# x kept in SBUF from the first attention into the cross attention of a decoder kernel

## The chip, the cores and the metric

The kernel runs on one core of a Trainium2 chip. The metric is the device time of one execution in microseconds. Times given as "median" are medians over several runs; the profile is of one further execution. Engines are called PE (TensorE, matmuls), PEld (its weight loads), DVE (VectorE), ACT (ScalarE), POOL (GpSimd) and SP (SyncE, which here only issues DMAs). Names such as SPq or PEq are an engine's instruction queue.

## What is computed

Two post-norm decoder layers over x of 8 x 256 rows with 512 columns, float32. Each step adds a branch to x and normalises the rows:

```
x = _layernorm(x + _L0_attn_ref(x, ...))        # quantised projections, 32 heads
x = _layernorm(x + _L0_xattn_ref(x, ctx_2048, mask))
x = _layernorm(x + _L0_ffn_ref(x, ...))         # base feed-forward and two of eight low-rank experts
x = _layernorm(x + _L1_attn_ref(x, ...))
x = _layernorm(x + _L1_xattn_ref(ctx, ctx, x, ...))
x = _layernorm(x + _L1_ffn_ref(x, ...))
```

The change lies in the end of the first line and in the second. The branch of the second line is one attention without projections, with D = 512:

```
scores = einsum('bsd,bmd->bsm', hidden_states, memory_tokens) * scale
scores = where(memory_mask, scores, -1e30)
attn = softmax(scores, axis=-1)
readout = einsum('bsm,bmd->bsd', attn, memory_tokens)
```

## The kernel before

The program is a list of stages, each a block in which the five engines run their own instruction lists and meet through semaphores. Between two stages all engines wait for each other. Every engine takes its list strictly in order, and a wait holds everything behind it on that engine. The order is written out by hand in loops, so the code order is the execution order of an engine. The 2048 rows of x are 16 tiles of 128 rows (NT = 16, index n); a block b of 256 rows has TB = 2 tiles.

**attention0_finish** (L710) is the last stage of the first attention: it quantises the attention's output cf, multiplies by the output weights, adds x and normalises. A loop over i works on block i, with these steps:

- POOL `take_bias` (L790) subtracts a bias from a block of cf, three blocks ahead; DVE `scale` (L850) multiplies it; ACT `rounded` (L916) adds the rounding constant; DVE `quantise` (L875) writes the bf16 operand quant, two blocks ahead.
- PE multiplies quant by the weights into one of four accumulators (L961, L966).
- DVE scales the accumulator of each tile into one of eight row buffers r (L890, signal y_ready), POOL adds x from a2_xt (L803, sum_ready), DVE takes mean and variance one block later (L904, L905, var_ready), POOL adds epsilon and takes the power -0.5 (L811, L813, root_ready), and DVE normalises the row in r two blocks later (L896, x1_ready).
- SP stores each finished row tile to the DRAM tensor x1 (L783). The stage ends when all stores have landed (L785).

In the trace the tiles a2_xt, a2_r and so on are called a_xt and a_r.

**cross_attention** (L1014) reads x1 back. A loop over s runs a pipeline over the tiles: at step s, PE transposes tile s of x (L1147, into c_pxf), multiplies scores of tile s-1 (L1156, c_psc), the output of tile s-3 (L1165, c_pout), and transposes the probabilities of tile s-2 (L1174, c_ppt), in this order. ACT copies the transposed x (L1186), takes the exponential of tile s-1 (L1193), copies the transposed probabilities of tile s-2 (L1200). DVE masks the scores of tile s-1 and takes their maximum (L1235 to L1238), adds the output of tile s-3 to x (L1249), takes its moments, and normalises tile s-4 (L1260). ACT also issues the stores of x2 (L1209).

SP feeds it: `load_x(b)` (L1090) issues three DMAs for block b, all counted on one semaphore got_x: x from x1 (L1094), the context rows ct (L1096) and the transposed context cf (L1098). There are three buffers, so blocks 0 to 2 are loaded at the start, and a later block b is issued at step 2b-2, once the tile two before it in DVE's additions is done (semaphore added). PE waits for all three DMAs ahead of the transposes of a block's first tile (L1143).

Beside this work the stage prepares the next stage's weights: 20 pieces, each loaded by SP into one of five raw buffers (L1113), rounded to a high part by ACT (L1205) and turned into a low part by DVE (L1265). `pieces_of(s)` (L1037) says which pieces belong to step s: `n * NT // NP == s`, which gives pieces 0 and 1 to step 0 and the last one to step 15. ACT and DVE take a step's pieces at the step's end; the piece that uses the same raw buffer five pieces on is issued by SP after w_low.

Of the kernel before, what the change touches and what calls it, by code (L numbers as in the profile page):

```python
# [15 lines left out]
F32 = mybir.dt.float32  # L16
# [6 lines left out]
P = 128  # L23
# [34 lines left out]
class Maker:  # L58
# [5 lines left out]
    def sb(self, name, shape, dt=F32):  # L64
        return self.ctx.enter_context(self.nc.sbuf_tensor(name, shape, dt))
# [644 lines left out]
def attention0_finish(nc, io, sem, keep):  # L710
# [9 lines left out]
    SPAN = KT * NC  # L720

    with ExitStack() as ctx:
# [27 lines left out]
        xt = mk.sb("a2_xt", [P, NT, D])  # L750
# [7 lines left out]
                 "y_ready", "sum_ready", "tail_steps", "var_ready", "root_ready", "x1_ready")  # L758
        s_ = {n: sem(f"a2_{n}") for n in names}
        got_x = [sem(f"a2_got_x{b}") for b in range(B)]  # L760
        stored = [sem(f"a2_stored{n}") for n in range(RR)]
# [11 lines left out]
        with nc.Block() as block:  # L773
            @block.sync
            def _(sp):
# [5 lines left out]
                for n in range(NT):  # L781
                    sp.wait_ge(s_["x1_ready"], n + 1)
                    sp.dma_start(io["x1"][n * P:(n + 1) * P, :], r[:, n % RR, :]).then_inc(stored[n % RR], 16)  # L783
                for n in range(RR):
                    sp.wait_ge(stored[n], 16 * (NT // RR))  # L785

            @block.gpsimd
            def _(pool):
# [7 lines left out]
                for i in range(B + 1):  # L796
                    for q in range(TB):
                        n = i * TB + q
                        if n < NT:
# [3 lines left out]
                            pool.tensor_tensor(r[:, n % RR, :], r[:, n % RR, :], xt[:, n, :], ALU.add  # L803
# [3 lines left out]
                    for q in range(TB):  # L807
                        n = (i - 1) * TB + q
                        if 0 <= n < NT:
# [3 lines left out]
                            pool.tensor_tensor(stats[:, n, 9:10], stats[:, n, 8:9], keep["neghalf"][:, :], ALU.pow  # L813
                                               ).then_inc(s_["root_ready"], 1)

            @block.vector
            def _(dve):
# [63 lines left out]
                for i in range(B + 2):  # L881
                    if i + 2 < B:
                        scale(i + 2)
                    for q in range(TB):
                        n = i * TB + q
                        if 0 <= n < NT:
                            dve.wait_ge(s_["acc_done"], n + 1)
                            if n >= RR:
                                dve.wait_ge(stored[n % RR], 16 * (n // RR))
                            dve.scalar_tensor_tensor(r[:, n % RR, :], acc[n % RING][:, :], unit_tok[:, n:n + 1], wsrow[:, :],  # L890
                                                     ALU.mult, ALU.mult).then_inc(s_["y_ready"], 1)
                    for q in range(TB):
                        n = (i - 2) * TB + q
                        if 0 <= n < NT:
                            dve.wait_ge(s_["root_ready"], n + 1)
                            dve.tensor_scalar(r[:, n % RR, :], r[:, n % RR, :], stats[:, n, 6:7], stats[:, n, 9:10],  # L896
                                              ALU.subtract, ALU.mult).then_inc(s_["x1_ready"], 1)
                    if i + 2 < B:
                        quantise(i + 2)
                    for q in range(TB):  # L900
                        n = (i - 1) * TB + q
                        if 0 <= n < NT:
                            dve.wait_ge(s_["sum_ready"], n + 1)
                            tl.step(dve.bn_stats(stats[:, n, 0:6], r[:, n % RR, :]))  # L904
# [3 lines left out]
            def _(act):  # L908
# [23 lines left out]
                for b in range(1, B):  # L932
                    rounded(b)
# [80 lines left out]
def cross_attention(nc, io, sem, keep):  # L1014

    NT = N // P
    XT, CT, RAW, HALF = 6, 3, 5, DFF // 2  # L1020
    CUT = ((0, 6), (6, FT))
    ER = E_ * R_
    BLOCKED = 1e30
# [2027 lines left out]
```

## Time and profile before

| | us |
|---|---|
| median of 3 runs | 2139.03 |
| lowest and highest of them | 2136.92, 2142.73 |
| the profiled execution: its time | 2141.15 |
| its span in the trace | 2139.4 |

| engine | busy us | share of the span |
|---|---|---|
| PE | 1819.8 | 85% |
| DVE | 1452.1 | 68% |
| ACT | 956.3 | 45% |
| POOL | 509.6 | 24% |

The shares are means over stages that have different limits. The stages that the change touches, by the trace: attention0_finish from 394.2 to 487.1 us, cross_attention from 487.1 to 615.4 us of the span. A timeline row reads: start, length, engine, source line, operation, what it wrote and read, shapes, count, and in square brackets how long the engine had been idle before it and what ended that. A merged row (x2) spans several instructions.

### The profile page before, as it was taken

Reading aid. Unit: us, or ns where it says so; the run is one execution under the profiler, and the core shown is the slowest. Engines: PE = TensorE matmul, PEld = TensorE weight load, DVE = VectorE, ACT = ScalarE, POOL = GpSimd, SP = SyncE. Lnnn points to the kernel's source line nnn. Section 1 sums busy time; section 2 is a strip of 40 time slices with the busy share of each in tenths; the row PEclk is TensorE's granted clock in tenths of the full one; section 3 lists DMA queues with packets and bytes.
Section 4 is the critical chain, followed back from the end, with each engine's and each line's share of the span. In section 5 each row is a group of like instructions: output and inputs, shape, how many; then the busy total and the mean of one; then the engine's idle time right before and its main releaser. Section 6 shows DMA issues by size and latency. Waiting matters only on the chain. (4 is left out here: it accounts for less than half of the span.)

```text
span 2139.4 us, 32688 instructions
## 1 busy us (share of the span) xinstructions
PE 1819.8 (85%) x12270; PEld 1374.9 (64%) x12270; DVE 1452.1 (68%) x2729; ACT 956.3 (45%) x1614; POOL 509.6 (24%) x503
## 2 busy tenths in 40 slices
PE   4489999765668999999999985999997799857886
PEld 2256665213448999999999975777875577623443
DVE  8478887694745566566566554566665677648997
ACT  3436666402314444444444432433443211259995
POOL 5233331270010010010000001001100388723422
PEclk9679999656889999999999997999998999978998
DMA  5598894217622122222221214211211311030000
GB/s 157 51 98 96 96 97 45 99 66 230 205 79 57 55 64 69 75 67 63 80 72 56 67 48 162 104 70 40 90 60 54 118 50 50 21 123 6 20 22 34
DMA packets 117568, 166.53 MB, mean 78 GB/s; under 512 B 13536, under 2 KB 67680, under 8 KB 115104
## 3 DMA queue, kind: packets, MB, share of 16 engines
q1 hardware_dynamic: 110756, 151.85, 29.9%
q10 hardware_dynamic: 6656, 12.58, 1.6%
q8 instruction: 99, 1.62, 0.4%
q14 instruction: 57, 0.47, 0.1%
HBM read 117.91 MB, written 21.05 MB: 65 GB/s over the span
## 5 line engine op out<-in xcount | busy, mean ns | idle before, releaser
L1583 ACT ACTIVATE f_gate<-f_gu 128x256 f32<-128x256 f32 x264 | 98.2, 381 | 274.3 <-PE f_gu L1449 187.1
L1711 DVE TENSOR_TENSOR f_hid<-f_gate,f_gu 128x256 f32<-128x256 f32 x264 | 108.2, 420 | 162.6 <-ACT f_gate L1583 159.7
L567 DVE TENSOR_REDUCE a_rowmax<-a_ring 128x2 f32<-128x512 f32 x256 | 164.9, 687 | 51.7 <-PE a_ring L649 49.4
L2525 PE MATMUL e_py<-e_kv,e_toep 128*128 128x320 f32 x640 | 174.5, 436 | 7.5 <-DVE e_kv L2549 7.5
L2525 PEld LDWEIGHTS e_py<-e_kv,e_toep 128*128 128x128 f32 x640 | 122.7, 192 | 59.0 <-issue 9.1
L520 ACT ACTIVATE a_prob<-a_sT 128x1024 f32<-128x1024 f32 x128 | 130.6, 1026 | 48.0 <-PE a_sT L638 48.0
L1462 PE MATMUL f_gu<-f_lowh,f_bg 128*128 128x256 f32 x704 | 141.3, 283 | 5.2 <-POOL f_lowl L1368 4.9
L1449 PE MATMUL f_gu<-f_xhi,f_wg 128*128 128x256 f32 x704 | 130.5, 283 | 0.0
L1449 PE MATMUL f_gu<-f_xhi,f_wu 128*128 128x256 f32 x704 | 129.1, 281 | 0.0
L1716 DVE TENSOR_TENSOR f_hl<-f_hid,f_hh 128x768 fp32r<-128x768 f32 (+2 forms) x90 | 84.5, 939 | 55.9 <-ACT f_hh L1629 54.8
L1462 PEld LDWEIGHTS f_gu<-f_lowh,f_bg 128*128 128x128 f32 x704 | 115.6, 191 | 9.7 <-POOL f_lowl L1368 5.2
L1486 PE MATMUL f_pout<-f_wd,f_hh 128*128 128x512 f32 x352 | 111.6, 398 | 0.0
L1449 PEld LDWEIGHTS f_gu<-f_xhi,f_wg 128*128 128x128 f32 x704 | 108.9, 189 | 0.9 <-POOL f_xlo L1364 0.8
L1449 PEld LDWEIGHTS f_gu<-f_xhi,f_wu 128*128 128x128 f32 x704 | 107.8, 188 | 0.0
L2017 PE MATMUL d_ring<-d_xh,d_w 128*128 128x256 f32 x512 | 95.9, 288 | 13.1 <-DVE d_xl L2336 13.1
L1629 ACT ACTIVATE f_hh<-f_hid 128x768 fp32r<-128x768 f32 (+2 forms) x90 | 74.9, 832 | 62.4 <-DVE f_hid L1711 62.4
L1462 PE MATMUL f_gu<-f_lowl,f_bg 128*128 128x256 f32 x352 | 99.5, 283 | 0.0
L1449 PE MATMUL f_gu<-f_xlo,f_wg 128*128 128x256 f32 x352 | 99.4, 283 | 0.0
L1449 PE MATMUL f_gu<-f_xlo,f_wu 128*128 128x256 f32 x352 | 99.0, 281 | 0.0
L649 PE MATMUL a_ring<-a_ks,a_qs 48*128 48x256 f32 x512 | 62.8, 322 | 40.4 <-DVE a_rowmax L567 20.2
L2017 PEld LDWEIGHTS d_ring<-d_xh,d_w 128*128 128x128 f32 x512 | 79.5, 192 | 20.0 <-issue 18.0
L481 POOL TENSOR_TENSOR a_y<-a_y,cb 128x512 f32<-128x512 f32 x48 | 50.0, 1042 | 177.2 <-DVE a_y L549 177.2
(420 smaller groups left out, 4853.5 us busy)
## 6 DMA issues: line engine op xcount, KB each, us to landing
f_entry<-in_WdT SPq DMA_DIRECT2D x89, 256.0 KB
d_staging<-in_w SPq DMA_DIRECT2D x16, 1024.0 KB, 5.5
a_qs<-a_hi SPq DMA_DIRECT2D x64, 128.0 KB, 7.2
a_ks<-a_hi SPq DMA_DIRECT2D x64, 128.0 KB, 6.2
e_toep<-lags SPq DMA_DIRECT2D x32, 256.0 KB, 3.1
f_entry<-in_Bg SPq DMA_DIRECT2D x89, 64.0 KB
f_entry<-in_Bu SPq DMA_DIRECT2D x89, 64.0 KB
cf<-in_xT SPq DMA_DIRECT2D x4, 1024.0 KB, 7.8
```

Source lines behind the costliest of these rows:

```text
L520: act.activation(prob[:, n % 4, :, :, :], sT[n % 2][:, :, :, :], ACT.Exp).then_inc(exp_done, 1)
L567: dve.tensor_reduce(rowmax[:, s % 2, :, e * SLOTS + j], ring[n % RING][:, :].rearrange("p (q t) -> p q t", t=T), AX.X, ALU.max, negate=Tru ...
L649: last = pe.matmul(dst[e][:, q * T:(q + 1) * T], qs[par][rows, pair, q * P:(q + 1) * P], ks[par][rows, pair, :], start=True, stop=True)
L1449: last = pe.matmul(gu[n % 3][:, w, :], ws[hw][:, k, f * P:(f + 1) * P], xs[:, b % 2, k, :], start=(m == 0 and w == 0), stop=(m == 3 * KT - ...
L1462: last = pe.matmul(gu[n % 3][:, w, :], bg[:, n % BR, h, w, :], xs[:, u, j - 1, w, :], start=False, stop=True, skip_group_check=True)
L1486: last = pe.matmul(pout[q][:, :], xs[:, t % 2, 0, cols], wd[:, n % WR, h, :], start=(f == 0 and m == 0), stop=(f == FT - 1 and m == 2))
L1583: act.activation(gate[:, i % 2, :], gu[n % 3][:, 0, :], ACT.Silu).then_inc(s_["gate_ready"], 1)
L1629: act.activation(hh[:, t % 2, lo:hi, :], hid[:, lo:hi, :], ACT.Copy).then_inc(s_["hh_ready"], 1)
L1711: dve.tensor_tensor(hid[:, j, :], gate[:, i % 2, :], gu[n % 3][:, 1, :], ALU.mult).then_inc(s_["hid_ready"], 1)
L1716: dve.tensor_tensor(hl[:, t % 2, lo:hi, :], hid[:, lo:hi, :], hh[:, t % 2, lo:hi, :], ALU.subtract).then_inc(s_["hl_ready"], 1)
L2017: last = pe.matmul(dst[:, f * T:(f + 1) * T], w[hw][:, wi, k, o * P:(o + 1) * P], xs[:, k, :], start=(m == 0), stop=(m == 3 * KT - 1))
L2525: last = pe.matmul(py[n % RING][:, 0:DIAG * BS], toep[:, h % 3, (t - j) * P:(t - j + 1) * P], kv[:, h % 2, :, j, :], start=(j == 0), stop= ...
```

## The change

1. **x stays in SBUF.** The buffer of x in attention0_finish becomes `x_rows1`, allocated so that it outlives the stage, and is handed on in `keep["rows1"]`. POOL's sum is written into it, not into r. Nothing is stored to x1, and cross_attention reads, updates and stores its tiles in this buffer; c_xt and c_r go. `load_x` issues two DMAs, not three.
2. **Where PE waits.** The wait for a block's DMAs moves from ahead of the transposes of its first tile to ahead of its scores, which are one step later.
3. **ScalarE makes the rows.** In attention0_finish the normalisation leaves DVE (L896) for ACT, as one activation with a scale and a bias per row. For the bias, -mean times root, POOL gets a third small operation per tile behind its power. DVE's wait for a row buffer is now on sum_ready, not on a landed store.
4. **Weight pieces two steps on.** `pieces_of` spreads the same 20 pieces over steps 2 to 15 and not over steps 0 to 15.

```
@@ attention0_finish
-                for n in range(NT):
-                    sp.wait_ge(s_["x1_ready"], n + 1)
-                    sp.dma_start(io["x1"][n * P:(n + 1) * P, :], r[:, n % RR, :]).then_inc(stored[n % RR], 16)
-                for n in range(RR):
-                    sp.wait_ge(stored[n], 16 * (NT // RR))
...
-                            pool.tensor_tensor(r[:, n % RR, :], r[:, n % RR, :], xt[:, n, :], ALU.add
+                            pool.tensor_tensor(xt[:, n, :], r[:, n % RR, :], xt[:, n, :], ALU.add
...
                             pool.tensor_tensor(stats[:, n, 9:10], stats[:, n, 8:9], keep["neghalf"][:, :], ALU.pow
+                                               ).then_inc(s_["root_steps"], 1)
+                            pool.wait_ge(s_["root_steps"], n + 1)
+                            pool.tensor_scalar(stats[:, n, 8:9], stats[:, n, 6:7], stats[:, n, 9:10], -1.0, ALU.mult, ALU.mult
                                                ).then_inc(s_["root_ready"], 1)
...
-                                dve.wait_ge(stored[n % RR], 16 * (n // RR))
+                                dve.wait_ge(s_["sum_ready"], n - RR + 1)
...
-                    for q in range(TB):
-                        n = (i - 2) * TB + q
-                        if 0 <= n < NT:
-                            dve.wait_ge(s_["root_ready"], n + 1)
-                            dve.tensor_scalar(r[:, n % RR, :], r[:, n % RR, :], stats[:, n, 6:7], stats[:, n, 9:10],
-                                              ALU.subtract, ALU.mult).then_inc(s_["x1_ready"], 1)
...
-                for b in range(1, B):
-                    rounded(b)
+                rounded(1)
+                for i in range(B + 2):
+                    if i + 2 < B:
+                        rounded(i + 2)
+                    for q in range(TB):
+                        n = (i - 2) * TB + q
+                        if 0 <= n < NT:
+                            act.wait_ge(s_["root_ready"], n + 1)
+                            act.activation(xt[:, n, :], xt[:, n, :], ACT.Identity, bias=stats[:, n, 8:9], scale=stats[:, n, 9:10]
+                                           )
@@ cross_attention
-        return [n for n in range(NP) if n * NT // NP == s]
+        return [n for n in range(NP) if 2 + n * (NT - 2) // NP == s]
...
-                    sp.dma_start(xt[:, at:at + TB, :], io["x1"][b * T:(b + 1) * T, :].rearrange("(n p) f -> p n f", p=P)
-                                 ).then_inc(got_x[b % CT], 16)
...
-                        pe.wait_ge(got_x[n // TB % CT], 48 * (n // TB // CT + 1))
                         if n >= 2:
                             pe.wait_ge(s_["xf_ready"], n - 1)
...
                         pe.wait_ge(s_["xf_ready"], n + 1)
+                        pe.wait_ge(got_x[n // TB % CT], 32 * (n // TB // CT + 1))
```

The instruction order of DVE in a middle iteration of the loop in attention0_finish (cf is the attention's output, a_r the row buffers). Before:

```order
L850 TENSOR_TENSOR cf<-cf,a_inv 128x4x256
L890 SCALAR_TENSOR_TENSOR a_r<-a_acc,a_unit_tok,a_wsrow 128x512 x2
L896 TENSOR_SCALAR a_r<-a_r,a_stats 128x512 x2
L875 SCALAR_TENSOR_TENSOR quant<-cf,a_grow 128x4x256
L904 BN_STATS a_stats<-a_r 128x6
L905 BN_AGGR a_stats<-a_stats 128x2
L904 BN_STATS a_stats<-a_r 128x6
L905 BN_AGGR a_stats<-a_stats 128x2
```

and of the change, the same place (x_rows is the kept buffer):

```order
L849 TENSOR_TENSOR cf<-cf,a_inv 128x4x256
L889 SCALAR_TENSOR_TENSOR a_r<-a_acc,a_unit_tok,a_wsrow 128x512 x2
L874 SCALAR_TENSOR_TENSOR quant<-cf,a_grow 128x4x256
L897 BN_STATS a_stats<-x_rows 128x6
L898 BN_AGGR a_stats<-a_stats 128x2
```

The two normalisations between the scaled accumulators and the quantisation are gone from DVE. POOL in the same iteration, of the change:

```order
L799 TENSOR_TENSOR x_rows<-a_r,x_rows 128x512 x2
L786 TENSOR_TENSOR cf<-cf,a_cbias 128x4x256
L807 TENSOR_SCALAR a_stats<-a_stats 128x1
L809 TENSOR_TENSOR a_stats<-a_stats,neghalf 128x1
L812 TENSOR_SCALAR a_stats<-a_stats 128x1
L807 TENSOR_SCALAR a_stats<-a_stats 128x1
L809 TENSOR_TENSOR a_stats<-a_stats,neghalf 128x1
L812 TENSOR_SCALAR a_stats<-a_stats 128x1
```

Here only the two operations of L812 are new. ACT at the start of cross_attention (c_xf is the transposed x, c_raw a raw weight buffer, f_wa and f_ad high parts of weights). Before:

```order
L1186 ACTIVATE c_xf<-c_pxf 128x512
L1205 ACTIVATE f_wa<-c_raw 128x512 x2
L1186 ACTIVATE c_xf<-c_pxf 128x512
L1193 ACTIVATE c_prob,c_rowsum<-c_score,c_negmax 128x256
L1205 ACTIVATE f_ad<-c_raw 128x768
```

and of the change:

```order
L1184 ACTIVATE c_xf<-c_pxf 128x512 x2
L1191 ACTIVATE c_prob,c_rowsum<-c_score,c_negmax 128x256
L1184 ACTIVATE c_xf<-c_pxf 128x512
L1191 ACTIVATE c_prob,c_rowsum<-c_score,c_negmax 128x256
L1198 ACTIVATE c_probT<-c_ppt 128x256
L1203 ACTIVATE f_wa<-c_raw 128x512 x2
L1184 ACTIVATE c_xf<-c_pxf 128x512
```

The first two weight pieces now stand behind the second tile's exponential, where before they stood behind the first copy of x.

## Rows read from the trace of the kernel before

**Rows 1.** Windows by stretch: length, busy of each engine, clock, DMA share, GB/s.
```profile
core 0: us, PE busy (x) PEld busy (x) DVE busy (x) ACT busy (x) POOL busy (x), PEclk, DMA share, GB/s
417.00:467.30 50.30, 40.12 (x82) 12.37 (x80) 43.07 (x51) 5.96 (x6) 38.40 (x35) 0.50 0.11 42
487.10:508.20 21.10, 6.34 (x21) 4.61 (x21) 2.21 (x5) 2.34 (x4) 0.00 (x0) 0.58 1.00 310
520.80:601.90 81.10, 59.80 (x216) 41.10 (x214) 60.15 (x163) 27.01 (x62) 8.20 (x12) 0.85 0.56 182
```

**Rows 2.** Timeline of DVE, one iteration of attention0_finish.
```profile
451.50 1.40 DVE L890 SCALAR_TENSOR_TENSOR a_r<-a_acc,a_unit_tok,a_wsrow 128x512 f32<-128x512 f32 x2
...
455.27 2.92 DVE L875 SCALAR_TENSOR_TENSOR quant<-cf,a_grow 128x1024 bf16<-128x1024 f32 x1
458.11 0.68 DVE L904 BATCH_NORM_STATS2 a_stats<-a_r 128x6 f32<-128x512 f32 x1
...
459.72 1.19 DVE L850 TENSOR_TENSOR cf<-cf,a_inv 128x1024 f32<-128x1024 f32 x1
460.83 1.41 DVE L890 SCALAR_TENSOR_TENSOR a_r<-a_acc,a_unit_tok,a_wsrow 128x512 f32<-128x512 f32 x2
462.15 2.53 DVE L896 TENSOR_SCALAR a_r<-a_r,a_stats 128x512 f32<-128x512 f32 x2
464.61 1.21 DVE L875 SCALAR_TENSOR_TENSOR quant<-cf,a_grow 128x1024 bf16<-128x1024 f32 x1
```

**Rows 3.** Timeline of POOL, the same iteration.
```profile
455.03 2.08 POOL L790 TENSOR_TENSOR cf<-cf,a_cbias 128x1024 f32<-128x1024 f32 x1
459.10 0.22 POOL L811 TENSOR_SCALAR a_stats<-a_stats 128x1 f32<-128x1 f32 x1 [1.99 <-DVE a_stats L905]
...
459.95 1.04 POOL L811 TENSOR_SCALAR a_stats<-a_stats 128x1 f32<-128x1 f32 x1
...
461.72 2.67 POOL L803 TENSOR_TENSOR a_r<-a_r,a_xt 128x512 f32<-128x512 f32 x2
```

**Rows 4.** Timeline at the two borders of attention0_finish.
```profile
394.24 0.06 DVE L820 MEMSET a_plus<- 128x1 f32 x1 [0.34 <-PEq L450]
...
483.02 0.55 DVE L896 TENSOR_SCALAR a_r<-a_r,a_stats 128x512 f32<-128x512 f32 x1 [0.45 <-POOL a_stats L813]
...
487.14 0.37 SPq L1094 DMA_DIRECT2D c_xt<-x  x1
```

**Rows 5.** Timeline, start of cross_attention; last, ACT's rounding by line, 417 to 467.3 us.
```profile
494.96 1.97 PE L1147 MATMUL c_pxf<-ident,c_xt 128*128 128x128 f32 x8 [23.09 <-DMA c_cf<-in_ctxFM]
496.76 3.78 PE L1156 MATMUL c_psc<-c_cf,c_xf 128*128 128x256 f32 x8
506.03 0.63 ACT L1205 ACTIVATE f_wa<-c_raw 128x512 fp32r<-128x512 f32 x1 [9.32 <-DMA c_raw<-in_AgT]
508.20 0.42 DVE L1235 SCALAR_TENSOR_TENSOR c_score<-c_psc,c_mask 128x256 f32<-128x256 f32 x1
...
L916 ACT ACTIVATE cf<-cf,a_plus 128x1024 f32<-128x1024 f32 x6 | 6.9, 1148 | 42.0 <-DVE cf L850 42.0
```

**Rows 6.** Cross_attention's steps: timeline; waits and one line of 520.8 to 601.9 us; a window.
```profile
520.76 0.42 DVE L1235 SCALAR_TENSOR_TENSOR c_score<-c_psc,c_mask 128x256 f32<-128x256 f32 x1
523.17 0.38 SPq L1094 DMA_DIRECT2D c_xt<-x  x1
529.87 1.12 PE L1147 MATMUL c_pxf<-ident,c_xt 128*128 128x128 f32 x4 [4.26 <-DMA c_cf<-in_ctxFM]
601.92 0.42 DVE L1235 SCALAR_TENSOR_TENSOR c_score<-c_psc,c_mask 128x256 f32<-128x256 f32 x1
...
DVE c_score L1235 <- PE c_psc L1156: 15.9, 5, 4.9
...
L1265 DVE TENSOR_TENSOR f_wu<-c_raw,f_wu 128x704 fp32r<-128x704 f32 x8 | 7.0, 884 | 0.0
...
520.00:525.00 5.00, 5.00 (x22) 3.25 (x21) 4.75 (x14) 2.71 (x6) 0.64 (x1) 1.00 0.37 90
```

More of the change, by code:

```diff
@@ L62, in __init__, with sb @@
         self.nc, self.ctx = nc, ctx
-    def sb(self, name, shape, dt=F32):
-        return self.ctx.enter_context(self.nc.sbuf_tensor(name, shape, dt))
+    def sb(self, name, shape, dt=F32, side="left"):
+        return self.ctx.enter_context(self.nc.sbuf_tensor(name, shape, dt, side=side))
     def ps(self, name, shape, dt=F32):
@@ L720, in attention0_finish @@
     SPAN = KT * NC
+    held = ExitStack()
+    xt = Maker(nc, held).sb("x_rows1", [P, NT, D], side="right")
+    keep["rows1"].update(held=held, rows=xt)
     with ExitStack() as ctx:
@@ L757, in attention0_finish @@
                  "bias_ready", "inv_ready", "cb_ready", "cbpart_ready", "eps_added", "sub_ready", "mul_ready", "round_ready", "quant_ready", "acc_done",
-                 "y_ready", "sum_ready", "tail_steps", "var_ready", "root_ready", "x1_ready")
+                 "y_ready", "sum_ready", "tail_steps", "var_ready", "root_steps", "root_ready")
         s_ = {n: sem(f"a2_{n}") for n in names}
         got_x = [sem(f"a2_got_x{b}") for b in range(B)]
-        stored = [sem(f"a2_stored{n}") for n in range(RR)]
         flat = keep["cf"][:, :, :].rearrange("p k (c t) -> p k c t", t=CHUNK)
@@ L880, in _ @@
                 quantise(1)
-                for i in range(B + 2):
+                for i in range(B + 1):
                     if i + 2 < B:
@@ L903, in _ @@
                             dve.wait_ge(s_["sum_ready"], n + 1)
-                            tl.step(dve.bn_stats(stats[:, n, 0:6], r[:, n % RR, :]))
+                            tl.step(dve.bn_stats(stats[:, n, 0:6], xt[:, n, :]))
                             dve.bn_aggr(stats[:, n, 6:8], stats[:, n, 0:6]).then_inc(s_["var_ready"], 1)
@@ L978, in attention0 @@
         mk = Maker(nc, ctx)
+        keep["rows1"] = {}
         own = dict(keep, ws=mk.sb("ws", [P, 4 * KT]), unit=mk.sb("unit", [P, NC]),
@@ L1019, in cross_attention @@
     NT = N // P
-    XT, CT, RAW, HALF = 6, 3, 5, DFF // 2
+    CT, RAW, HALF = 3, 5, DFF // 2
+    xt = keep["rows1"]["rows"]
     CUT = ((0, 6), (6, FT))
@@ L1037, in pieces_of @@
     def pieces_of(s):
-        return [n for n in range(NP) if n * NT // NP == s]
-    with ExitStack() as ctx:
+        return [n for n in range(NP) if 2 + n * (NT - 2) // NP == s]
+    with keep["rows1"]["held"], ExitStack() as ctx:
         mk = Maker(nc, ctx)
-        xt = mk.sb("c_xt", [P, XT, D])
         ct = mk.sb("c_ct", [P, CT, TB, D])
@@ L1068, in cross_attention @@
         got_x = [sem(f"c_got_x{u}") for u in range(CT)]
-        stored = [sem(f"c_stored{u}") for u in range(4)]
+        stored = sem("c_stored")
         piece_in = [sem(f"c_piece_in{u}") for u in range(RAW)]
@@ L1146, in _ @@
                         for k in range(KT):
-                            last = pe.transpose(pxf[n % 2][:, k * P:(k + 1) * P], xt[:, n % XT, k * P:(k + 1) * P],
+                            last = pe.transpose(pxf[n % 2][:, k * P:(k + 1) * P], xt[:, n, k * P:(k + 1) * P],
                                                 keep["ident"][:, :])
@@ L1208, in _ @@
                         act.wait_ge(s_["x_ready"], n + 1)
-                        act.dma_start(io["x2"][n * P:(n + 1) * P, :], r[:, n % 4, :]).then_inc(stored[n % 4], 16)
-                for n in range(4):
-                    act.wait_ge(stored[n], 16 * (NT // 4))
+                        act.dma_start(io["x2"][n * P:(n + 1) * P, :], xt[:, n, :]).then_inc(stored, 16)
+                act.wait_ge(stored, 16 * NT)
             @block.vector
@@ L1257, in _ @@
                     if 0 <= n < NT:
-                        y = r[:, n % 4, :]
+                        y = xt[:, n, :]
                         dve.wait_ge(s_["root_ready"], n + 1)
```

9 lines of the change are left out of this document (2 added, 7 removed).

## The prediction

> **What bounds the kernel now.** I read the windows first [rows 1], cut at the borders of the two stages that the change touches, then the timelines in them, last the list of waits. Everything after 615.4 us has the same instructions in both kernels, so the sum is made of three stretches only.
>
> In the loop of attention0_finish (417 to 467.3 us) no engine is full: DVE is busy for 43.1 of 50.3 us, POOL for 38.4, PE for 40.1 at half its clock [rows 1]. But an iteration takes 460.83 - 451.50 = 9.33 us [rows 2], and some of the busy time is waiting in disguise. The quantisation L875 took 2.92 us where it ran beside POOL's L790 and 1.21 us where it did not; POOL's tiny L811 took 1.04 us beside DVE's L850 and 0.22 us alone [rows 2, 3]. The starts fit one reading: these operations do not run side by side. L790 ended at 457.11, and the quantisation ended 1.08 us later, at 458.19, as if it had begun then. L904 (one SBUF input) and L890 (which reads PSUM) kept their short times. So POOL and part of DVE take turns, and the loop is bound by a chain that crosses both.
>
> At the start of cross_attention (487.1 to 508.2 us) nothing computes much: DVE 2.2 of 21.1 us, DMA share 1.00 [rows 1]. PE waits for the first block until 494.96. Then ACT waits 9.32 us for the first weight piece, to 506.03, and the first scores wait on DVE behind that piece, to 508.20 [rows 5]. In the body (520.8 to 601.9 us) DVE is busy for 60.15 of 81.1 us [rows 1] and waits 15.9 us in five waits for scores; PE had stood before the transposes of a block's first tile for its DMAs, 4.26 us in one case [rows 6], with the previous tile's scores queued behind them.
>
> **Loop of attention0_finish.** The two normalisations leave DVE: 2.53 us in rows 2, of which most is turn-taking with L803. The freed time does not all come out. POOL's own work in an iteration is the two sums 2.5 (2.67 with a short turn in them), L790 1.9 (2.08 with one), two roots at 0.85 each = 1.7 (from 459.10 to 459.95) [rows 3]. New are two operations like L811, 0.22 us and a gap of 0.08, 0.6 together. To this come DVE's turns for L850 and L875, each about 1.15 us, in which POOL stands: 2.5 + 1.9 + 1.7 + 0.6 + 2.3 = 9.0 us. POOL had 1.99 us of idle time in the iteration, waiting for DVE's variance [rows 3]; that goes, and POOL becomes the bound at 9.0 against 9.33. I take 0.35 us for each of four iterations, 1.4 us.
>
> How far the turns reach is the open question of this stretch, since the sum for POOL rests on them: with turns 9.0 us, without them 6.7 (the second rival). The trace has both operations that waited for another's end (the 2.92 and the 1.04 us) and none of these kinds that ran through, so I take the turns. The Trainium skill, page "SBUF — State Buffer", section "Who interferes with whom", has a rule for this: a DVE instruction with two SBUF inputs or in a 2-port mode and a GpSimd instruction that reads SBUF exclude each other, and the one that comes second blocks until the first has finished. By that rule the change is partly against itself, as it takes 16 short instructions of DVE out of the queue for the port and puts 16 of GpSimd in, each of which can stand for a whole turn of DVE's; the loop's gain would then be the 1.4 us above and not the rival's 16.
>
> Behind the last quantisation the loop drains. From 460.8 us the last norm ends at 483.57, 22.8 us later [rows 2, 4]. In the change POOL has left: the rest of one pair of roots 2.1, one quantisation's turn 1.1, three pairs of sums 7.5, four pairs of roots at 2.3 = 9.2, then ACT's last row 0.6: 20.5 us. So the drain gives 2.2 us. ACT's row of 512 is priced from its 1.15 us for 1024 columns [rows 5] at 0.6 us; 2 x 0.6 + 1.15 per iteration leaves it idle most of the time, and only the last row is on the path.
>
> The border: 483.57 to 487.14 = 3.6 us, the last store's landing and the meeting of the engines. A border with no store took 0.34 us [rows 4]. It gives between 2.5 and 3.2 us; I take 3. Together 1.4 + 2.2 + 3 = **7 us** (4 to 10: at the low end the loop gives nothing).
>
> **Start of cross_attention.** PE needs no DMA for its transposes now. The first scores need ct and cf of block 0: 1.0 MB and not 1.5 MB. At the stretch's mean rate of 310 GB/s [rows 1] 0.5 MB is 1.7 us, of which I take 1.4, since part of it overlapped other transfers; so they land at 6.4 us after the stage's start and not at 7.8. Scores take 3.8 us at the cold clock [rows 5]: first scores on DVE at 10.3 us, before at 21.1. The pieces no longer stand in front. Three x loads less (1.5 MB) bring the first two pieces in by 4 us or more: ACT had them at 18.9 us, now near 15, and step 2 asks for them at 15.5 to 16.5. Two pieces in step 2 cost about 1.6 us of DVE that step 0 paid in its wait before. Step 4 then begins near 23.6 us, before at 520.76 - 487.14 = 33.6 us [rows 6]. **10 us** (8 to 12, by the pieces and the block landing 2 us later or earlier than this).
>
> **Body of cross_attention.** Steps 4 to 16 took 601.92 - 520.76 = 81.2 us, 6.8 us each [rows 6]. The load of block 3 is issued at 523.17 and complete at 529.87, and PE wanted it at 525.6. In the change PE runs the transposes at once, then the scores of tile 5, and meets the wait only a step later, near 531. There the block has landed, the more so as x no longer travels in front of it (1.4 us). So the wait is moved to where its slack is 1 to 3 us, and what waits behind it on PE is the output of tile 4, which DVE wants about 2 us after its scores. What is late next is DVE itself: 60.15 us of work, plus two pieces that now fall into these steps (17 and not 15) at 0.88 = 61.9 us [rows 1, 6]. In an unhindered window DVE was busy 4.75 of 5 us [rows 6]: 61.9 / 0.95 = 65.2 us, 5.4 us per step. PE needs at most 5.0 us per step by its busy time, 59.8 / 12, part of it at a lower clock. 81.2 - 65.2 = 16 us. I take **15 us** (9 to 17), one microsecond being left for late blocks. The end from step 16 on is unchanged: no pieces there, the same stores.
>
> **Sum.** 7 + 10 + 15 = 32 us. From the profiled execution, 2141.15 (span 2139.4 and 1.75 around it), this gives 2109.2. The median of the runs is 2.1 us lower, so 2107.
>
> **Rivals.**
>
> *The wait is moved, not removed.* PE stops before the scores of each block's first tile instead. For it: only 1 to 3 us of slack, and the DMAs share their engines with pieces that are issued in bursts. Against it: the missing x, and one full step of 5.4 us gained. If each of the five waits of 15.9 us keeps 2 us, the body gives 6 and the sum is 23: 2116. Chance 0.15.
>
> *The turns do not bind.* If GpSimd's small operations slip between DVE's and DVE's own work is the bound, a loop iteration falls from 9.33 to POOL's 6.7 us (2.5 + 1.9 + 1.7 + 0.6): 2.6 us in six iterations = 16 and not 4, sum 44: 2095. Against it: the 1.04 us of a 0.22 us instruction. Chance 0.07.
>
> *The new start is not taken.* The pieces are still what step 2 waits for, if SP's queue is held by its issues and the first pieces land near 19 us as before. Then step 2's DVE waits 3 to 4 us more, and with it some late blocks: start 5, body 9, sum 21: 2118. Chance 0.08.
>
> *Slower: ScalarE's rows set the loop.* The trace shows no activation of ACT with a scale and a bias per row, in place. If one costs X us, ACT's iteration is 1.15 + 2X and it holds the rounding of the next block behind it, so PE's operand. It binds from 1.15 + 2X = 9.0, X = 3.9 us. To eat the 32 us in eight iterations each must grow by 4 us, so X = 5.9 us is the point from which the kernel is slower than before; at X = 7 an iteration is 15.2 us and the time 2107 + 8 x 6.2 = 2156. The nearest rows, 0.6 to 0.63 for 512 columns [rows 5], are ten times smaller. Chance 0.03.
>
> **How the numbers follow.** Forecast 2107 (its own bounds: 4 + 8 + 9 = 21 to 10 + 12 + 17 = 39 us, 2100 to 2118) 0.64, the rivals 0.15, 0.07, 0.08, 0.03; 0.03 for a change of no more than a few microseconds whatever the cause. The range 2099 to 2119 takes in the forecast's bounds and the rivals at 2116 and 2118, and leaves out the ones at 2095 and 2156. A measurement of this kernel can tell about 0.3%, 6.4 us, from no change. Faster than that: all cases but the last two, 0.93; within it 0.04; slower 0.03.
>
> **What would show each step.** In the changed profile: the last ACT row of attention0_finish near 480 us and the first SP issue of cross_attention less than 1.2 us behind it; POOL without idle time in the loop, iterations of 9.0 us; first scores on DVE about 10.3 us after the stage's start; step 4 at 23.6 us; steps of 5.4 us, with DVE busy 95% and hardly a PE wait for a DMA; PE's clock at its upper level through the body, where before it fell with each wait (0.85 in rows 1). Wrong would be: waits of PE for cf at L1154 of more than 1 us each, a loop iteration under 8 us or over 9.5, or an ACT row of over 1 us.

## The result and the profile after

| | before | after |
|---|---|---|
| median, us | 2138.2 (4 runs) | 2109.0 (4 runs) |
| lowest and highest | 2136.9, 2142.7 | 2107.1, 2110.5 |
| profiled execution: time, span | 2141.15, 2139.4 | 2108.64, 2106.7 |

The ratio is 0.9867, with a 95% interval from 0.9851 to 0.9883. The time fell by 29 us by the medians and by 32.7 us between the two profiled executions, of which that of before is one of its slower ones (2141.15, where its median is 2138.2). The prediction was 2107.

Windows by stretch, of after: one of the loop, one of the start of cross_attention, one of its steps 4 to 16. The columns are those of [rows 1].

```profile
core 0: us, PE busy (x) PEld busy (x) DVE busy (x) ACT busy (x) POOL busy (x), PEclk, DMA share, GB/s
417.30:463.70 46.40, 39.43 (x81) 12.21 (x80) 28.89 (x43) 11.93 (x13) 40.09 (x40) 0.50 0.00 0
482.90:492.00 9.10, 5.71 (x19) 4.55 (x20) 0.95 (x4) 1.19 (x2) 0.00 (x0) 0.51 0.82 263
504.70:569.30 64.60, 52.33 (x206) 33.29 (x205) 61.42 (x166) 27.25 (x64) 8.20 (x12) 0.97 0.60 199
```

Against [rows 1], DVE has emptied in the loop (28.9 us of work), while POOL is busy for 40.1 of 46.4 us, where it was 38.4 of 50.3. The stretch from stage start to the first scores is 9.1 us and not 21.1. The body is 64.6 us and not 81.1, DVE is busy for 95% of it, and PE's granted clock there is 0.97 and not 0.85.

An iteration of the loop, DVE, of after; it answers to [rows 2].

```profile
449.74 1.22 DVE L849 TENSOR_TENSOR cf<-cf,a_inv 128x1024 f32<-128x1024 f32 x1 [3.50 <-POOL cf L786]
450.88 1.40 DVE L889 SCALAR_TENSOR_TENSOR a_r<-a_acc,a_unit_tok,a_wsrow 128x512 f32<-128x512 f32 x2
452.20 1.22 DVE L874 SCALAR_TENSOR_TENSOR quant<-cf,a_grow 128x1024 bf16<-128x1024 f32 x1
...
458.54 1.22 DVE L849 TENSOR_TENSOR cf<-cf,a_inv 128x1024 f32<-128x1024 f32 x1 [3.50 <-POOL cf L786]
```

POOL in the same iteration; it answers to [rows 3].

```profile
447.81 1.89 POOL L786 TENSOR_TENSOR cf<-cf,a_cbias 128x1024 f32<-128x1024 f32 x1
449.79 1.25 POOL L807 TENSOR_SCALAR a_stats<-a_stats 128x1 f32<-128x1 f32 x1
451.13 0.57 POOL L809 TENSOR_TENSOR a_stats<-a_stats,neghalf 128x1 f32<-128x1 f32 x1
451.80 0.26 POOL L812 TENSOR_SCALAR a_stats<-a_stats 128x1 f32<-128x1 f32 x1
452.14 0.22 POOL L807 TENSOR_SCALAR a_stats<-a_stats 128x1 f32<-128x1 f32 x1
452.44 1.39 POOL L809 TENSOR_TENSOR a_stats<-a_stats,neghalf 128x1 f32<-128x1 f32 x1
453.93 0.26 POOL L812 TENSOR_SCALAR a_stats<-a_stats 128x1 f32<-128x1 f32 x1
454.16 2.49 POOL L799 TENSOR_TENSOR x_rows<-a_r,x_rows 128x512 f32<-128x512 f32 x2
456.61 1.89 POOL L786 TENSOR_TENSOR cf<-cf,a_cbias 128x1024 f32<-128x1024 f32 x1
```

An iteration is 8.80 us (447.81 to 456.61). POOL waits for nobody in it (between its operations stand only gaps of up to 0.10 us), and DVE waits 3.50 us for POOL's subtraction. The tiny L807 takes 1.25 us where DVE's L849 started 0.05 us ahead of it, and 0.22 us 2.4 us later; L809 takes 1.39 us over DVE's L874 and 0.57 us otherwise. Those are the two turns of the prediction, 1.03 and 0.82 us.

The border into cross_attention, of after (against [rows 4]):

```profile
480.59 0.26 POOL L812 TENSOR_SCALAR a_stats<-a_stats 128x1 f32<-128x1 f32 x1
480.88 0.81 ACT L933 ACTIVATE x_rows<-x_rows,a_stats 128x512 f32<-128x512 f32 x1 [0.49 <-POOL a_stats L812]
482.93 0.37 SPq L1094 DMA_DIRECT2D c_ct<-in_ctx  x1
```

The start of cross_attention, of after (against [rows 5]):

```profile
482.99 1.94 PE L1144 MATMUL c_pxf<-ident,x_rows 128*128 128x128 f32 x8 [14.71 <-PEq L3028]
488.23 3.70 PE L1154 MATMUL c_psc<-c_cf,c_xf 128*128 128x256 f32 x8 [3.30 <-DMA c_cf<-in_ctxFM]
...
491.96 0.42 DVE L1232 SCALAR_TENSOR_TENSOR c_score<-c_psc,c_mask 128x256 f32<-128x256 f32 x1 [0.28 <-PE c_psc L1154]
...
497.40 0.63 ACT L1203 ACTIVATE f_wa<-c_raw 128x512 fp32r<-128x512 f32 x1 [1.03 <-DMA c_raw<-in_AgT]
```

PE transposes at once and stops once for a DMA, 3.30 us, for the context. The first scores stand at 491.96, 9.03 us after the stage's start at 482.93. ACT takes the first weight piece at 497.40 and has waited 1.03 us for it, not 9.32.

Waits in the body of after (engine, tile, line, releaser: us in total, times, longest):

```profile
POOL c_stats L707 <- DVE c_stats L701: 57.0, 12, 5.8
ACT c_prob L1191 <- DVE c_negmax L1235: 37.2, 12, 3.6
PEld c_pout L1163 <- ACT c_probT L1198: 16.7, 11, 2.4
PE c_pout L1163 <- ACT c_probT L1198: 12.3, 11, 2.0
```

No wait for a DMA is left in the list and no wait of DVE, whose 15.9 us of waits for scores [rows 6] are gone. POOL and ACT wait for DVE, and PE for ACT's copy, which stands behind that exponential.

### The profile page after: what moved, and what is told of

Same layout as the page of the kernel before. It is cut to its first block and busy times, and to the rows that moved or that the text cites. A ratio compares the mean times of both kernels' runs of the same rounds, so it can differ in the third digit from the quotient of the medians.

```text
span 2106.7 us, 32643 instructions
## 1 busy us (share of the span) xinstructions
PE 1805.1 (86%) x12252; PEld 1365.3 (65%) x12270; DVE 1433.8 (68%) x2713; ACT 968.4 (46%) x1630; POOL 515.2 (24%) x519
## 5 line engine op out<-in xcount | busy, mean ns | idle before, releaser
L2520 PEld LDWEIGHTS e_py<-e_kv,e_toep 128*128 128x128 f32 x640 | 122.6, 192 | 59.1 <-issue 9.1
```

The costliest lines, as they stand in the source:

```text
L2520: last = pe.matmul(py[n % RING][:, 0:DIAG * BS], toep[:, h % 3, (t - j) * P:(t - j + 1) * P], kv[:, h % 2, :, j, :], start=(j == 0), stop= ...
```

## The experiments

Every kernel is read in the same three stretches of its one trace, each measured from inside the stage, since the stages before shift by a microsecond or two from run to run. Rows that do not begin with "before" are edits of after. "Finish": from the first scaled accumulator (416.96 us in before) to cross_attention's first DMA issue. "Start": from there to the scores of step 4. "Body": steps 4 to 16.

| kernel | median us | ratio, 95% | finish | start | body |
|---|---|---|---|---|---|
| before | 2138.2 | 1 | 70.2 | 33.6 | 81.2 |
| after | 2109.0 | 0.9851 to 0.9883 | 66.1 | 21.8 | 64.5 |
| rows back on DVE | 2110.5 | 0.9857 to 0.9887 | 67.9 | 21.8 | 64.5 |
| pieces from step 0 | 2112.8 | 0.9875 to 0.9910 | 66.1 | 28.1 | 63.0 |
| wait at the transposes | 2111.4 | 0.9862 to 0.9891 | 66.1 | 21.6 | 68.2 |
| before, split wait | 2123.7 | 0.9917 to 0.9947 | 70.2 | 33.2 | 63.7 |
| before, pieces from step 2 | 2131.9 | 0.9951 to 0.9975 | 70.2 | 26.0 | 78.3 |
| DVE op of two inputs | 2110.8 | 0.9849 to 0.9889 | 68.6 | 22.5 | 64.8 |
| DVE op of one input | 2108.1 | 0.9838 to 0.9870 | 63.8 | 22.4 | 64.8 |
| ACT rows in both stages | 2102.0 | 0.9809 to 0.9845 | 66.1 | 22.1 | 59.1 |
| ... and epsilon on DVE | 2094.7 | 0.9776 to 0.9810 | 57.7 | 21.7 | 59.0 |
| ... and roots by pair | 2093.7 | 0.9772 to 0.9808 | 58.1 | 21.0 | 59.0 |

How far can these numbers be trusted? Where two kernels have the same code in a stretch, the traces agree: finish is 66.07 to 66.09 us in four of them and 70.18 to 70.21 in three, and start and body of after, the rows on DVE and the two dummy operations lie within 0.7 and 0.3 us. Everything outside the three stretches took between 1952 and 1956 us, so medians and profiles can differ by a few microseconds for reasons that lie elsewhere. The ratios are against before as measured again beside each kernel (medians 2138.0, 2139.3 and 2139.7 us). Differences to before need more care: its start and body come from one trace of an execution 3 us above its median, and where these 3 us lie is not known. So a gain against before that is read from stretches may be up to 3 us too large.

**The rows back on DVE.** The change without its third part: in attention0_finish DVE normalises x_rows in place, and POOL's third operation goes.

```
-                            pool.wait_ge(s_["root_steps"], n + 1)
-                            pool.tensor_scalar(stats[:, n, 8:9], stats[:, n, 6:7], stats[:, n, 9:10], -1.0, ...)
...
+                            dve.tensor_scalar(xt[:, n, :], xt[:, n, :], stats[:, n, 6:7], stats[:, n, 9:10],
+                                              ALU.subtract, ALU.mult)
```

> The changed kernel with the normalisation of attention0_finish back on DVE and POOL's third small operation per tile gone; x stays in SBUF, nothing is stored. Theory (POOL and DVE take turns and POOL's chain is the bound in the changed loop; most of this stage's 4.2 us came from the store that no longer has to land): iterations return to 9.3 us, the last row ends near 483.5 us, cross_attention's first DMA is issued about 1.2 us later, near 484.7 against 482.9: 2 us slower than the changed kernel, 2111. Rival (ScalarE's rows brought the stage's gain): 4 us slower, 2113, and the next stage starts near 487.

Finish took 67.9 us, 1.8 more than after, as expected; the medians differ by 1.5 us, within their spread. Of the three parts that were taken back one by one, ScalarE's rows are the smallest. The remaining 2.3 us of this stage's gain are the border: from the last row to SP's first issue it is 1.24 us here too, with no store.

**The pieces from step 0.** The change without its fourth part.

```
-        return [n for n in range(NP) if 2 + n * (NT - 2) // NP == s]
+        return [n for n in range(NP) if n * NT // NP == s]
```

> The changed kernel with the weight pieces spread over steps 0 to 15 as before. Theory (the piece in step 0 holds ACT and DVE until its DMA lands): the first piece lands 14.5 us after the stage's start as in the changed kernel, first scores at 16.5 us and not at 9.0, step 4 near 28 us and not 21.8; in the body two pieces less, 1.8 us given back: 5 us slower, 2114. Rival (the removed x loads made the start): first scores at 9 to 10 us all the same, 2108 to 2110.

ACT stands before the first piece again, now with nothing else to wait for:

```profile
493.75 0.63 ACT L1203 ACTIVATE f_wa<-c_raw 128x512 fp32r<-128x512 f32 x1 [11.68 <-DMA c_raw<-in_AgT]
```

The first scores come 15.6 us after the stage's start and not 9.0; step 4 at 28.1 and not 21.8. The body is 1.5 us shorter, because two pieces fewer fall into it (15 and not 17), near the 1.8 us of their DVE work. So the shift gives 6.3 and takes 1.5. The median rose by 3.8 us, to 2112.8 where 2114 was expected.

**The wait back at the transposes.** The change without its second part.

```
                     n = s
                     if n < NT:
+                        pe.wait_ge(got_x[n // TB % CT], 32 * (n // TB // CT + 1))
...
-                        pe.wait_ge(got_x[n // TB % CT], 32 * (n // TB // CT + 1))
```

> The changed kernel with PE's wait for ct and cf back ahead of the transposes of a block's first tile; x is in SBUF and not loaded. Theory (the wait's place does it: queued behind it are the scores of the tile before): PE waits about 4 us in each of five blocks, falls to the lower clock, DVE waits about 2 us each time: body 10 us longer (5 to 12), start 1 us later, 2119. Rival (the missing x load made the blocks early enough): 0 to 2 us, 2110.

This was a miss: the body grew by 3.7 us, not by 10, and the median is 2111.4. PE's stops are 2.6 us on the mean and not the expected 4. Waits in its body:

```profile
PE c_pxf L1145 <- DMA c_cf<-in_ctxFM: 13.0, 5, 3.3
...
DVE x_rows L1244 <- PE c_pout L1163: 1.9, 3, 1.0
DVE c_score L1232 <- PE c_psc L1154: 1.6, 3, 0.9
```

PE's timeline at the first two stops:

```profile
510.28 0.82 PE L1145 MATMUL c_pxf<-ident,x_rows 128*128 128x128 f32 x4 [3.34 <-DMA c_cf<-in_ctxFM]
510.89 3.46 PE L1154 MATMUL c_psc<-c_cf,c_xf 128*128 128x256 f32 x8
...
522.36 0.66 PE L1145 MATMUL c_pxf<-ident,x_rows 128*128 128x128 f32 x4 [1.97 <-DMA c_cf<-in_ctxFM]
522.85 1.89 PE L1154 MATMUL c_psc<-c_cf,c_xf 128*128 128x256 f32 x8
```

and the windows of the scores behind each:

```profile
510.90:514.30 3.40, 3.40 (x10) 2.75 (x10) 2.50 (x9) 0.60 (x1) 0.55 (x1) 0.54 0.29 111
522.90:524.70 1.80, 1.80 (x11) 1.59 (x10) 1.69 (x8) 0.66 (x2) 0.55 (x1) 1.00 0.62 236
```

For comparison, the scores behind a stop in before:

```profile
530.77 3.62 PE L1156 MATMUL c_psc<-c_cf,c_xf 128*128 128x256 f32 x8
```

In before PE's five stops in the body were 3.5 to 4.8 us, 21.3 in all, and DVE waited 15.9 us for scores behind them and 2.0 us for the output matmuls, 17.9 together. With no x to load they are 2.0 to 3.3 us, 13.0 in all, and DVE waits 1.6 and 1.9, 3.5 together, near the 3.7 us by which the body grew. So a stop of 2.6 us costs DVE 0.7, and one of 4.3 us costs it 3.6.

There is a second cost behind a stop: slow scores. Eight score matmuls take 1.89 us at a granted clock of 1.00, the upper level (2.4 GHz). Behind the five stops of before they took 2.8 to 3.6 us, 1.3 more on the mean. Here it depends on the stop: behind those of 1.97 and 2.02 us the clock was 1.00 and the scores took 1.89 us; behind those of 2.73, 2.97 and 3.34 us it was 0.59, 0.72 and 0.54 (partly the lower level, 1.2 GHz), and they took 3.10, 2.74 and 3.46 us, which makes 0.7 more on the mean of the five. Stop plus slow scores, less what DVE waited, is PE's lead: 4.3 + 1.3 - 3.6 = 2.0 us in before and 2.6 + 0.7 - 0.7 = 2.6 us here. That is an estimate from means; single stops give leads between 2 and 4 us.

**The split wait alone.** Before, with x's load on a semaphore of its own: PE waits for x at the transposes and for ct and cf at the scores. Everything else is as in before.

```
-                                 ).then_inc(got_x[b % CT], 16)
+                                 ).then_inc(got_r[b % CT], 16)
...
-                        pe.wait_ge(got_x[n // TB % CT], 48 * (n // TB // CT + 1))
+                        pe.wait_ge(got_r[n // TB % CT], 16 * (n // TB // CT + 1))
...
                         pe.wait_ge(s_["xf_ready"], n + 1)
+                        pe.wait_ge(got_x[n // TB % CT], 32 * (n // TB // CT + 1))
```

> The kernel before with one edit: x has a semaphore of its own, the transposes wait for x alone and the scores, one step later, for ct and cf. x is still stored and loaded. Theory (the wait's place does it): x, issued first, lands about 2 us before cf, PE's wait shrinks from 4.5 to 1.5 us and DVE's to almost none, body 14 us shorter; the start stays held by the first piece: 2124 to 2126. Rival (x must be resident): body shorter by 3 us at most, 2135.

The body fell by 17.5 us with x still going through DRAM; 14 were expected, and by the medians it is 14.3. PE now stops for x, which comes first of the three; its body's list of waits says

```profile
PE c_pxf L1148 <- DMA c_xt<-x: 9.2, 5, 3.3
```

which is 1.8 us per stop and within PE's lead: DVE waits 0.7 us in the whole body. Together with the run before this it shows that the old place of the wait costs much only while the stops are long. The wait's place alone takes 17.5 us off the body of before; the other three parts of the change, with the wait in its old place, 12.9 us; all four together 16.6 us. (The last two carry 1.5 us for the two pieces more.) The gains do not add: 17.5 and 12.9 are nearly twice the 16.6, and a body of before that is read 3 us too long would not change that. How much of the 12.9 is due to x in SBUF is not shown by itself, since no run has it alone; the next run has the pieces alone.

**The pieces alone.** Before with part 4 only.

> The kernel before with one edit: the weight pieces spread over steps 2 to 15. Theory: first scores at about 13.5 us after the stage's start and not at 21.1; the first pieces still land at 18.9 us, behind three x loads, and step 2 waits for them; step 4 at 26 us and not 33.6; in the body the two more pieces fall into DVE's waits: 6 us faster, 2132. Rival (the x loads are what makes the start late): 0 to 2 us faster, 2137.

The start gained 7.6 us, the first scores standing at 12.9 us and not 21.1; the median, 2131.9, is the expected one. The body gained 2.8 us in spite of two pieces more: DVE waited 11.9 us for scores and 1.6 for outputs, 4.4 less than in before. So of the 12.9 us just named the pieces can have brought some 3, which leaves about 10 for x in SBUF, as an estimate that takes the two to add.

**Do the turns exist?** The change, with one dummy operation per loop iteration added on DVE behind the variances, where DVE is idle and POOL runs its sums and its subtraction. Two kernels, both reading 1024 columns: one with two SBUF inputs, one with one. (`row` stands for wsrow, a tile in SBUF, read twice over. The second operation also writes only two columns.)

```
+                    if 1 <= i <= 5:
+                        ex.step(dve.tensor_tensor(spare[:, :, :], row, row, ALU.add))
...
+                    if 1 <= i <= 5:
+                        ex.step(dve.tensor_reduce(spare[:, 0, 0:2], row, AX.X, ALU.max))
```

> The changed kernel with an extra DVE operation of 128 x 1024 with two SBUF inputs, about 1.1 us, in each of five iterations of attention0_finish, where DVE is idle for 3.5 us; its result is not used. Theory (turns, POOL's chain the bound): POOL stands for it, iterations 9.9 us and not 8.8: 5.5 us slower, 2114.5. Rival (no turns; DVE has the time): iterations 8.8 us, 2109.

> The same with an extra DVE reduction of 128 x 1024 elements, one SBUF input, about 1.1 us, in the same place. Theory (turns exist only for two SBUF inputs or the fast modes): hidden in DVE's idle time, iterations 8.8 us, 2109. Rival (any DVE work in this place delays the loop, by its order): as in the run with two inputs, 2114.

The timelines of DVE and of POOL, with two inputs:

```profile
446.14 2.13 DVE L902 TENSOR_TENSOR a_spare<-a_wsrow 128x1024 f32<-128x1024 f32 x1
450.13 1.24 DVE L850 TENSOR_TENSOR cf<-cf,a_inv 128x1024 f32<-128x1024 f32 x1 [1.86 <-POOL cf L787]
...
447.15 2.88 POOL L787 TENSOR_TENSOR cf<-cf,a_cbias 128x1024 f32<-128x1024 f32 x1
```

and with one:

```profile
445.08 1.19 DVE L902 TENSOR_REDUCE a_spare<-a_wsrow 128x2 f32<-128x1024 f32 x1
448.10 1.24 DVE L850 TENSOR_TENSOR cf<-cf,a_inv 128x1024 f32<-128x1024 f32 x1 [1.82 <-POOL cf L787]
...
446.10 1.89 POOL L787 TENSOR_TENSOR cf<-cf,a_cbias 128x1024 f32<-128x1024 f32 x1
448.07 0.23 POOL L808 TENSOR_SCALAR a_stats<-a_stats 128x1 f32<-128x1 f32 x1
448.39 1.37 POOL L810 TENSOR_TENSOR a_stats<-a_stats,neghalf 128x1 f32<-128x1 f32 x1
```

With two inputs L902 stands 1.0 us until POOL's sums have ended (447.18), then POOL's subtraction stands 1.0 us for L902. With one input both run through, in the middle of POOL's sums. An iteration is 9.22 us in the first and 8.24 in the second: one turn, 0.98 us. The turns are shown. That the second input makes the difference, and not the 1024 columns written, is told by another operation: DVE's L889, which has one tensor in SBUF and one in PSUM as inputs and writes 512 columns to SBUF, keeps its 0.7 us each in after (450.88) while POOL's power and product run in their 0.57 and 0.26 us. The Trainium skill, page "SBUF — State Buffer", section "Who interferes with whom", says that a DVE operation with two SBUF inputs and a GpSimd operation that reads SBUF exclude each other, while a DVE operation with one SBUF input, outside the 2-port modes, doesn't contend; both runs agree with it.

What neither theory had is that the second kernel's loop is faster than that of the change, with more work in it (finish 2.2 us shorter; the medians are 0.9 us apart, within their spread). Both expectations missed by it: iterations of 8.8 us were expected with one input and 9.9 with two. In after, POOL meets both turns of DVE with 1.03 + 0.82 = 1.85 us of standing. Here L808 starts 0.03 us ahead of DVE's L850 and runs through in 0.23 us, the power L810 stands for 0.80 us (1.37 against 0.57) and the product L813 for 0.49 (0.75 against 0.26): 1.29 us. So 0.56 us per iteration hangs on which of two requests comes first. The kernel with two inputs meets the same order, and its iteration is 8.80 - 0.56 + 0.98 = 9.22 us. Why DVE's start is 0.1 us behind POOL's end here and 0.04 in after stays open.

**ScalarE's rows in both stages.** The change, and its third part done in cross_attention too: DVE's L1255 leaves for ACT, POOL gets a third small operation per tile.

> The changed kernel with part 3 done in cross_attention too: DVE's normalisation of each tile goes to ACT, POOL gets the third small operation there. Theory (DVE is the bound of the body at 5.4 us per step, ACT and POOL have room): 0.46 us per step less, body 5.5 us shorter, the last row 0.6 us later: 2104. Rival (PE, at 4.7 us of work per step with its chain through ACT, is as near): 1 to 2 us faster, 2108.

The body's window:

```profile
504.00:563.00 59.00, 51.89 (x206) 32.60 (x205) 55.83 (x153) 36.95 (x76) 17.50 (x24) 1.00 0.68 218
```

DVE lost 5.6 us of work and the body 5.5 us, as expected (the median, 2102.0, is 2 us below the expected one); DVE is still 95% busy. So in the body DVE's work is the bound, and what leaves DVE there is time saved one for one, unlike in the loop of attention0_finish.

**Epsilon on DVE.** The kernel just above, and in attention0_finish one POOL operation per tile moved to DVE.

```
-                            pool.tensor_scalar(stats[:, n, 8:9], stats[:, n, 7:8], EPS, None, ALU.add).then_inc(s_["eps_added"], 1)
-                            pool.wait_ge(s_["eps_added"], n + 1)
...
-                            dve.bn_aggr(stats[:, n, 6:8], stats[:, n, 0:6]).then_inc(s_["var_ready"], 1)
+                            tl.step(dve.bn_aggr(stats[:, n, 6:8], stats[:, n, 0:6]))
+                            dve.tensor_scalar(stats[:, n, 8:9], stats[:, n, 7:8], EPS, None, ALU.add).then_inc(s_["var_ready"], 1)
```

> The kernel with ScalarE's rows in both stages, and in attention0_finish the addition of epsilon moved from POOL to DVE (one more operation of 128x1 per tile there, one less on POOL). Theory, POOL's chain is the bound of the loop and of the drain: a pair of roots shrinks by 2 x 0.32 = 0.64 us, an iteration from 8.80 to 8.16 us, and eight pairs make 5.1 us of the stage: first scaled accumulator to stage border 61 us, median 2097 us. Rival, the loop is bound elsewhere (DVE's chain, or PE at half its clock): the stage stays at 66 us and the median at 2102. Second rival, the turns move onto longer operations and POOL stands longer for each: 63.5 us, 2099.5.

POOL, one iteration:

```profile
446.22 0.54 POOL L807 TENSOR_TENSOR a_stats<-a_stats,neghalf 128x1 f32<-128x1 f32 x1
446.86 0.78 POOL L810 TENSOR_SCALAR a_stats<-a_stats 128x1 f32<-128x1 f32 x1
447.61 0.54 POOL L807 TENSOR_TENSOR a_stats<-a_stats,neghalf 128x1 f32<-128x1 f32 x1
448.25 0.26 POOL L810 TENSOR_SCALAR a_stats<-a_stats 128x1 f32<-128x1 f32 x1
448.47 3.48 POOL L799 TENSOR_TENSOR x_rows<-a_r,x_rows 128x512 f32<-128x512 f32 x2
451.91 1.90 POOL L786 TENSOR_TENSOR cf<-cf,a_cbias 128x1024 f32<-128x1024 f32 x1
```

The iteration is 7.56 us, where 8.16 was expected, and finish fell by 8.4 us, where 5.1 was expected. An operation of 0.22 us gave 0.45, with its semaphore: in the drain, where no turns fall on them, a pair of roots takes 1.70 us from the end of the sums before it to the start of the next, and took 2.60 in after. The rest is shorter turns, 0.52 + 1.00 us and not 1.85. The median fell by 7.3 us, to 2094.7 where 2097 was expected. POOL was the bound.

**Roots by pair.** As before it, and POOL takes the power and the product for both tiles at once; DVE adds epsilon and negates the mean for both.

> As the run before, and the roots of a pair of tiles in one go: DVE adds epsilon and negates the mean for both tiles at once (two operations of 128x2), POOL takes the power and the product for both at once (two operations and not six). A pair of roots then takes about 1.0 us of POOL and not 2.64. Theory, POOL's chain alone: 1.6 us per iteration, 7.2 us each. PE needs about 7.4 us per iteration at half its clock (40.1 us in 5.4 iterations of before), so I expect it to be late next, at 7.4 us: 1.4 us in each of six iterations and 1.6 us in each of two pairs of the drain, stage 54.5 us, median 2090. Rival, POOL was not the only bound: iterations stay over 8.1 us, the stage over 60 us, median 2096 or more.

POOL, one iteration:

```profile
446.07 3.47 POOL L799 TENSOR_TENSOR x_rows<-a_r,x_rows 128x512 f32<-128x512 f32 x2
449.50 1.89 POOL L786 TENSOR_TENSOR cf<-cf,a_cbias 128x1024 f32<-128x1024 f32 x1
451.64 1.58 POOL L807 TENSOR_TENSOR a_stats<-a_stats,neghalf 128x2 f32<-128x2 f32 x1 [0.24 <-DVE a_stats L900]
453.37 0.20 POOL L811 TENSOR_TENSOR a_stats<-a_stats 128x2 f32<-128x2 f32 x1
```

An iteration takes 7.45 us. My number was 7.4, but for a wrong reason: I took it from PE, and PE idles 1.45 us per iteration here, waiting for DVE's quantisation. POOL now waits for DVE's second small operation, and its turns have grown to 1.0 + 0.9 us. The stage did not get shorter than in the kernel before it (58.1 against 57.7 us), since in the drain POOL waits for DVE's pair. DVE itself waits for no other engine in an iteration. So the theory of that run, POOL's chain and then PE, is wrong, though its 7.4 us came; the rival's sentence, that POOL was not the only bound, holds, though its numbers (over 8.1 us, over 60 us) did not come: here the loop ends at a chain through both engines. These two kernels are the fastest of the study, 2094.7 and 2093.7 us, and can't be told apart.

## Why the prediction was right, point by point

| term | predicted, us | measured, us |
|---|---|---|
| loop of attention0_finish | 1.4 | 1.05 |
| its drain | 2.2 | 0.7 |
| border | 3 | 2.3 |
| start of cross_attention | 10 | 11.8 |
| body, steps 4 to 16 | 15 | 16.6 |
| sum (the first three rounded up to 7) | 32 | 32.5 |

The sum agrees because three terms came out small and two large; that the errors cancel to within a microsecond is luck. The measured column compares the two profiled executions. By the medians the fall is 29.2 us where 32 was forecast, and 2107 came within 2 us of 2109.0 also because it started from 2139, a microsecond above the median of four runs.

**The loop.** POOL is the bound, waiting for nobody, as forecast; the turns are real, so the rival at 2095 falls. Iterations are 8.80 and not 9.0 us: POOL's roots took more than I had summed, its turns less (1.85, not 2.3). The four iterations were not all at 9.33 before; from the third on they took 8.40, 9.73 and 9.33 us, and take 8.82, 8.79 and 8.80 now. That is 0.42 lost, then 0.94 and 0.53 won: 1.05.

**The drain.** From the last full iteration's scaled rows (459.68) to the end of the last row (481.69) it took 22.0 us, where the sum had 20.5. The mis-sized term is "four pairs of roots at 2.3": a tile's three tiny operations with their gaps take 1.32 us, not 1.15. The price of L812 was 0.22 + 0.08 from L811; it takes 0.26 and stands 0.10 behind the power and 0.08 ahead of the next operation. Per pair that is 2.6, over four pairs 1.2 us. The last row took 0.81 us and not 0.6: that price was half of the 1.15 us of 1024 columns with a bias alone, and this one has 512 columns with a scale and a bias per row. How the 0.2 us divide between the two differences is not shown.

**The border.** 1.24 us lie between the last row and SP's first issue. I had 3.6 - 3 = 0.6, the bounds 0.4 to 1.1, from a border where the next stage's first operation had waited 0.34 us; even the upper bound was too low.

**The start.** The context landed 5.3 us after the stage's start, not 6.4, the first scores came at 9.0 and not 10.3, and step 4 at 21.8 and not 23.6. So 1.3 us of the surplus were there at the first scores, most of it the context, and 0.5 came in steps 1 to 3, which the prediction did not work out one by one. The pieces landed in time (ACT waited 1.03 us), so the rival in which step 2 takes over their wait falls. The run with the pieces from step 0 shows the mechanism: 6.3 us of the 11.8 hang on the pieces. The other 5.5, which the prediction gave to the missing x loads and to PE's earlier transposes, were not taken apart.

**The body.** 65.2 us were worked out from DVE's work at 95% and 64.5 came, with DVE at 95.1%; I had kept 1 us back for late blocks, and there were none. PE's clock in it was at the upper level nearly throughout, as forecast. The rival in which the wait is moved but not removed falls: the body's waits have no DMA in them.

One argument held less than it seemed. I put the body's gain down mainly to the wait's new place. The runs show that the place alone does it, but that the other parts without it do most of it too, x in SBUF about 10 us by the estimate above, since a stop of 2.6 us is mostly covered by PE's lead and one of 4.3 is not. It was this that my expectation of the third run missed.

**ScalarE's rows.** 0.81 us each, far from the 5.9 of the slower rival. This part is worth 1.8 us.

## What to carry to other kernels

A stop on a feeding engine costs only what exceeds its lead, so two edits that each shorten the same stop don't add: price them together, from the lead. Once an engine has become the bound of a loop with tiny dependent operations, price each as its length plus its semaphore step, and move the smallest one off: here one addition per tile, moved to DVE, was worth 8.4 us of the stage (7.3 by the medians), over four times the 1.8 us of ScalarE's rows. A part of it was shorter turns, which nobody had forecast. An engine's busy time says what it would gain only where it is full, as DVE in the body (5.6 us of work less, 5.5 us of time less).

## What the runs showed of the hardware

- Operations of 128x1 on POOL stand for a whole turn of DVE's two-input operation on 1024 columns: 1.25 us and not 0.22. The other way it depends on the form: DVE's addition of epsilon on 128x1 took 0.15 us at 445.13 in the kernel with epsilon on DVE, beside POOL's subtraction; on 128x2, in the kernel with roots by pair, it took 1.21 us at 442.77, to the end of that subtraction, and 0.17 us without POOL beside it.
- More work on DVE made a loop faster: with a one-input operation of 1.19 us added, an iteration went from 8.80 to 8.24 us, and POOL's first root operation got in ahead of DVE's turn. Which of two requests comes first, 0.03 to 0.05 us apart, was worth 0.56 us per iteration.
- From the last operation of one stage to SP's first DMA issue of the next, a meeting of all engines with no transfer to wait for, it took 1.24 us, in after and in the kernel with the rows on DVE.
- A stop of PE can cost more than its length: behind 3.34 us without work it came back at a granted clock of 0.54 and took 3.46 us for eight score matmuls, and behind 1.97 us at 1.00 and took 1.89.
